# Features of keys and queries: one fp32 row-tile product of unsplit numbers in place of three terms of rounded parts

## What is computed

```python
q = einsum('bsd,dhk->bhsk', x, wq)      # 16 heads of 32; k and v alike
def _phi(u, omega):                     # omega: 128 x 32
    proj = einsum('bhsk,mk->bhsm', u, omega)
    sq = 0.5 * sum(u * u, axis=-1, keepdims=True)
    stab = max(proj, axis=-1, keepdims=True)
    return exp(proj - sq - stab) / sqrt(m) + 1e-06
pq, pk = _phi(q * scale, omega), _phi(k * scale, omega)
kv = einsum('bhsm,bhsk->bhmk', pk, v);  z = sum(pk, axis=2)
out = einsum('bhsm,bhmk->bhsk', pq, kv) / einsum('bhsm,bhm->bhs', pq, z)
```

## Time and profile before

| what | value |
|---|---|
| median of 3 runs | 3481.13 us (3478.57 to 3484.28) |
| the profiled execution, its span | 3482.2 us (1.1 us above the median, inside the three) |
| PE busy | 3422.0 us, 98% |
| weight loads (PEld) busy | 3151.9 us, 91% |
| DVE / ACT / POOL busy | 71% / 57% / 32% |
| mean granted TensorE clock | 0.993 of full speed |
| DMA queue's packets | 34.6% of 16 engines' span |

### The profile page before, as it was taken

One profiled execution on the slowest core, in us unless ns is written; L12 is line 12 of the kernel. 1 busy time (PEld: TensorE's weight loads), 2 busy tenths in 40 slices (PEclk: granted clock), 3 DMA queues, 4 the chain that ended last, 5 costly groups with the idle time before them and its releaser, 6 DMA issues.

```text
span 3482.2 us, 77456 instructions
## 1 busy us (share of the span) xinstructions
PE 3422.0 (98%) x29993; PEld 3151.9 (91%) x29993; DVE 2468.2 (71%) x4839; ACT 1969.8 (57%) x4240; POOL 1105.2 (32%) x861
## 2 busy tenths in 40 slices
PE   8999999999899999999999999999999999999998
PEld 6888888888788888888888889999999999999998
DVE  6767777677667777677777766666666666666666
ACT  6777777777556666666656654444444444444443
POOL 3554554545345454555555532000000000000000
PEclk9999999999899999999999999999999999999999
DMA  3222222222323333232332346444444444444443
GB/s 128 80 77 74 95 77 83 77 74 77 107 79 114 106 102 115 82 126 94 102 109 93 111 144 206 147 148 148 147 146 146 146 146 146 146 146 146 146 147 126
DMA packets 195355, 409.83 MB, mean 118 GB/s; under 512 B 27440, under 2 KB 52528, under 8 KB 194992
## 3 DMA queue, kind: packets, MB, share of 16 engines
q1 hardware_dynamic: 194992, 404.89, 34.6%
HBM read 292.50 MB, written 112.33 MB: 116 GB/s over the span
## 4 chain that ended last, share of the span: by engine, by line
PE 70%; DVE 2%; ACT 1%; issue 0%; POOL 0%; DMA 0%; ACTq 0%; POOLq 0%; DVEq 0%
PE ffn_hidden L175 30%; PE attend_gated L175 20%; PE ffn_result L175 8%; PE attend_num L175 6%; PE attend_feat L1425 3%; PE attend_feat L1445 1%; PE ffn_turn L1910 1%; PE attend_turn L1415 1%; DVE attend_kvz_lo L1393 1%; DVE attend_pT_lo L1354 1%; PE attend_feat L1452 1%; PE attend_turn L1434 0%; ACT attend_kvz_hi L1300 0%; DVE attend_kvz_lo L1396 0%; DMA ffn_r_in<-in_L_attn_w_dram 0%
## 5 line engine op out<-in xcount | busy, mean ns | idle before, releaser
L175 PE MATMUL ffn_hidden<-ffn_yT_hi,ffn_wa_hi 128*128 128x256 f32 x2048 | 574.1, 280 | 3.5 <-DVE ffn_wa_lo L1798 1.8
L175 PE MATMUL ffn_hidden<-ffn_yT_lo,ffn_wa_hi 128*128 128x256 f32 x2048 | 573.3, 280 | 0.0
L175 PE MATMUL ffn_hidden<-ffn_yT_hi,ffn_wa_lo 128*128 128x256 f32 x2048 | 572.0, 279 | 0.0
L316 POOL TENSOR_TENSOR ffn_n_rstd<-ffn_n_base,ffn_n_power 128x2 f32<-128x2 f32 x32 | 27.5, 860 | 1300.1 <-DVE ffn_n_negmean L311 1300.1
L1780 ACT ACTIVATE ffn_ht_hi<-ffn_hs 128x512 fp32r<-128x512 f32 x248 | 156.4, 631 | 420.6 <-DVE ffn_hs L1827 420.6
L175 PEld LDWEIGHTS ffn_hidden<-ffn_yT_hi,ffn_wa_hi 128*128 128x128 f32 x2048 | 385.0, 188 | 4.4 <-DVE ffn_wa_lo L1798 2.3
L175 PEld LDWEIGHTS ffn_hidden<-ffn_yT_hi,ffn_wa_lo 128*128 128x128 f32 x2048 | 385.2, 188 | 0.0
L175 PEld LDWEIGHTS ffn_hidden<-ffn_yT_lo,ffn_wa_hi 128*128 128x128 f32 x2048 | 384.9, 188 | 0.2
L635 POOL TENSOR_TENSOR keys_z_sum<-keys_z_sum,keys_e 128x512 f32<-128x512 f32 x192 | 259.6, 1369 | 232.9 <-ACT keys_e L703 232.9
L1831 DVE TENSOR_TENSOR ffn_ht_lo<-ffn_hs,ffn_ht_hi 128x512 fp32r<-128x512 f32 x248 | 173.6, 700 | 218.9 <-ACT ffn_ht_hi L1780 218.9
L1765 ACT ACTIVATE ffn_hid<-ffn_hidden,ffn_bias 128x256 f32<-128x256 f32 x496 | 206.1, 467 | 180.5 <-PE ffn_hidden L175 180.5
(11 more groups left out here) (305 smaller groups left out, 11669.3 us busy)
## 6 DMA issues: line engine op xcount, KB each, us to landing
ffn_tq<-part_d SPq DMA_DIRECT2D x248, 512.0 KB, 3.9
keys_xin<-in_L_attn_x_dram SPq DMA_DIRECT2D x32, 512.0 KB, 4.5
xn_d<-keys_xn SPq DMA_DIRECT2D x32, 512.0 KB, 3.0
xT_d<-keys_xT_whole SPq DMA_DIRECT2D x32, 512.0 KB, 2.6
u_d<-keys_uq SPq DMA_DIRECT2D x32, 512.0 KB, 3.1
shared_xTf<-xT_d SPq DMA_DIRECT2D x32, 512.0 KB, 6.0
shared_uq<-u_d SPq DMA_DIRECT2D x32, 512.0 KB, 4.9
r_d<-shared_gate SPq DMA_DIRECT2D x32, 512.0 KB, 3.1
```

What stands on the lines that cost most here:

```text
L175: last = pe.matmul(out, stationary[a], moving[b], start=start and n == 0, stop=stop and n == len(TERMS) - 1)
```

## The change

`kT`, `qT` and `omT` become single fp32 tensors. Each three-term product of features becomes one product of fp32 operands, with the same stationary and moving shapes and the same order over c and j. The turned keys are copied once, by DVE (a copy in the place of the subtraction, which now itself waits for the turn on PE and for the `proj` that read `kT` last); ACT's copy is gone. The turned queries are copied once, by ACT in its old place; DVE's subtraction is gone. `omT` is copied once. All other products stay as they are, L1452 (`pick`) too.

```diff
@@ ACT, keys pass
-            act.activation(omT.hi[:, :], turn[:, 0:M], ACT.Copy).then_inc(omega_rounded, 1)
+            act.activation(omT[:, :], turn[:, 0:M], ACT.Copy).then_inc(omega_ready, 1)
...
-                if job == "turn_k":
-                    for j in range(HC):
-                        wait(act, feat[j].full, TG * g)
-                    act.wait_ge(k_turned, 2 * g + n + 1)
-                    act.activation(kT.hi[:, 2 * n:2 * n + 2, :], turn_halves, ACT.Copy).then_inc(kT_hi, 1)
@@ DVE, keys pass
-            dve.wait_ge(omega_rounded, 1)
-            dve.tensor_tensor(omT.lo[:, :], turn[:, 0:M], f32(omT.hi[:, :]), ALU.subtract).then_inc(omega_ready, 1)
...
                 if job == "turn_k":
-                    dve.wait_ge(kT_hi, 2 * g + n + 1)
-                    dve.tensor_tensor(kT.lo[:, 2 * n:2 * n + 2, :], turn_halves,
-                                      f32(kT.hi[:, 2 * n:2 * n + 2, :]), ALU.subtract).then_inc(k_split, 1)
+                    for j in range(HC):
+                        wait(dve, feat[j].full, TG * g)
+                    dve.wait_ge(k_turned, 2 * g + n + 1)
+                    dve.tensor_copy(kT[:, 2 * n:2 * n + 2, :], turn_halves).then_inc(k_split, 1)
@@ PE, keys pass, job proj
-                        for k, (x_, y_) in enumerate(TERMS):
-                            for j in range(HC):
-                                last = pe.matmul(feat[j].t[:, c * M:(c + 1) * M],
-                                                 kT[rows(j), c, n * P:(n + 1) * P][x_], omT[rows(j), :][y_],
-                                                 start=k == 0, stop=k == 2)
+                        for j in range(HC):
+                            last = pe.matmul(feat[j].t[:, c * M:(c + 1) * M], kT[rows(j), c, n * P:(n + 1) * P],
+                                             omT[rows(j), :], start=True, stop=True)
@@ ACT, attend pass
-                    act.activation(qT.hi[:, 2 * n:2 * n + 2, :], turn_halves, ACT.Copy).then_inc(qT_hi, 1)
+                    act.activation(qT[:, 2 * n:2 * n + 2, :], turn_halves, ACT.Copy).then_inc(q_split, 1)
@@ DVE, attend pass
-                if job == "turn_q":
-                    dve.wait_ge(qT_hi, 2 * g + n + 1)
-                    dve.tensor_tensor(qT.lo[:, 2 * n:2 * n + 2, :], turn_halves, f32(qT.hi[:, 2 * n:2 * n + 2, :]),
-                                      ALU.subtract).then_inc(q_split, 1)
@@ PE, attend pass, job max: as proj, with qT; job feat:
-                        for k, (x, y_) in enumerate(TERMS):
-                            for j in range(HC):
-                                if c == 0 and k == 0:
-                                    pe.wait_ge(feat[j].free, 4 * g + 2 + n)
-                                pe.matmul(feat[j].t[:, cols], omT[rows(j), :][y_], qT[rows(j), 2 * n + c, :][x],
-                                          start=k == 0, stop=False)
+                        for j in range(HC):
+                            if c == 0:
+                                pe.wait_ge(feat[j].free, 4 * g + 2 + n)
+                            pe.matmul(feat[j].t[:, cols], omT[rows(j), :], qT[rows(j), 2 * n + c, :], start=True, stop=False)
```

More of the change, by code:

```diff
@@ L878, in do @@
                     for c in range(NC):
[L879 to L885 removed]
+                        for j in range(HC):
+                            last = pe.matmul(feat[j].t[:, c * M:(c + 1) * M], kT[rows(j), c, n * P:(n + 1) * P],
+                                             omT[rows(j), :], start=True, stop=True)
+                            if c == NC - 1:
+                                last.then_inc(feat[j].full, 1)
                 if job == "kv":
@@ L1420, in do @@
                     for c in range(NC):
[L1421 to L1429 removed]
+                        for j in range(HC):
+                            if c == 0:
+                                wait(pe, feat[j].free, 4 * g + n)
+                            last = pe.matmul(feat[j].t[:, c * M:(c + 1) * M], qT[rows(j), c, n * P:(n + 1) * P],
+                                             omT[rows(j), :], start=True, stop=True)
+                            if c == NC - 1:
+                                last.then_inc(feat[j].full, 1)
                 if job == "below":
```

70 lines of the change are left out of this document (28 added, 42 removed), and 6 rows, old and new, of tables (FFN_OVER, KEYS_OVER).

## The result

The changed kernel takes 3435.27 us (median of 4 runs, 3434.16 to 3437.23); the kernel before, on the same chip, 3482.7 us (4 runs, 3478.57 to 3487.75). The ratio is 0.9868, with a 95% interval of 0.9854 to 0.9882: 47.4 us less of the medians, 41 to 51 by the interval. Two later executions, both of the kernel with two copies (experiment 5), ran at a mean granted clock of 0.85 and 0.56 and took 3680 and 5528 us; they are left out of its median and ratio.

What follows compares the result with a forecast made beforehand. The prediction took PE's own instructions to bound the keys and attend passes. Its terms, -57.3 + 12.8 - 2.0 - 0.3 = -46.8 us from the profiled 3482.2 us, gave 3435.4, written as 3435 us, range 3402 to 3474.

Steps and rivals of the forecast that it cites:

- PE bounds both passes: In the keys and attend passes PE's own instructions set the time: busy 808 of 810 and 1084 of 1090 us.
- 128 columns, -57.3 us: `proj` and `max` (L881, L1425): a chunk costs 0.224 us in place of 0.336, over 512 chunks, -57.3 us.
- 256 columns, +12.8 us: `feat` (L1445): two fp32 records of 0.23 us make a chunk 0.46 in place of 0.36, over 128 chunks, +12.8 us.
- Copies and waits, -2.0 us: Keys pass: without ACT's copy the chain PE waits for shortens; of PE's 3.3 us of waits, 2 are given back.
- the start, -0.3: Start of the kernel: one small subtraction fewer, -0.3 us.
- Rival 1, pairs in single file: Row-tile products: strict program order makes a product's second record hold up the next head; +129 us, 3609 us, chance 0.13.
- Rival 2, the gain of `max` is not kept: Attend pass: waits for feature banks lose L1425's half of the 57.3 us; 3464 us, chance 0.10.
- Rival 3, 256 columns at 0.12 a record: `feat` (L1445): an fp32 record costs 0.12 us, not 0.23; 3407 us, chance 0.09.
- Rival 4, a chunk at 0.315 us: 128-column products: partly held up pairs at about 0.315 us a chunk leave no gain; 3482 us, chance 0.04.

Runs made afterwards that it cites:

- experiment 5: The changed kernel with ACT's copy of the turned keys back, into a buffer nothing reads, and DVE's copy waiting for it: 3439.38 us, ratio 0.9876.
- Experiments 1 and 2: 1: kernel before with only keys (`proj`) fp32, 3456.54 us. 2: changed kernel with keys pass as before, only queries (`max`, `feat`) fp32, 3458.11 us.
- experiment 3: The changed kernel with loops of `proj` and `max` exchanged, heads outside and chunks inside, eight records of a head in a row: 3648.8 us, ratio 1.0471.
- experiments 6 to 8: 6: kernel before, fp32 keys, `max` only hi by hi, 3420.92 us. On it, 7: second `r` before the turn, 3482.16; 8: second `max` before first `k`, 3474.61.
- experiment 4: The changed kernel with `proj` and `max` ordered as two chunks (four records) of each head in a row, then the other two: 3454.81 us, ratio 0.9918.

## Why the prediction was right, point by point

**The total** was right, 3435 against 3435.27, and the chance went where it belonged. That it came out to 0.3 us is luck. The two large terms were each too large: together they gave -44.5 us and measured -42.0. The copies and the start, for which 2.3 us were given, show no net gain. What closed the gap is 6.8 us that the sum did not have, more than half of it from the clock, which the sum took as unchanged. Also, 3435.4 was the sum for the profiled execution, which took 3433.4; less the 1.1 us that were named, it would have been 3434 for the median.

- *PE bounds both passes*. Right. PE's busy time and the span fell by the same 49 us.
- *128 columns, -57.3 us.* The mechanism is right, the size is 0.85 of it: 48.8. The step of 0.112 us is exact, eight in place of twelve. The term mis-sized is the entry: the pass was to be 8 x 0.112 + 0.24 = 1.14 us and is 1.19, since the first step of fp32 takes 0.214 us (491.616 to 491.830) where the first step of three terms took 0.16 (504.59 to 504.75). 0.052 us x 128 = 6.7 us, and the heads' 7 ns stagger makes 1 more. Experiments 1 and 2 show the term in its halves.
- *256 columns, +12.8 us.* 6.8 were measured. The record takes 0.217 to 0.224 us (1226.105 to 1226.329), so my 0.23 was 0.01 high, and a chunk costs 0.08 more, not 0.10: the second `feat` of a group is 2 x 0.08 longer (1.249 to 1.409). The first is only 0.08 longer (1.426 to 1.506); why it gives half of it back was not tried. The Trainium skill (FP8 and Floating Point Precision, Matmul Precision, TensorE Precision Notes) counts four passes for fp32; at 256 columns these records agree, two of 0.22 us to a product where an fp32r one takes 0.12. At 128 columns a product costs only twice an fp32r one, 0.224 against 0.112.
- *Copies and waits, -2.0 us, and the start, -0.3.* The term was mis-sized; as a net gain it does not show. By the list of waits 3.3 became 2.4 us for the keys, but the waits for `xT_lo` rose from 3.2 to 4.6. From the start to the 5th `proj` the change gains 0.4 us, where its passes alone are 1.2 shorter. Experiment 5 shows the price of a second copy in the changed kernel, 0.9 us in the trace and 3 to 4 in the medians, all that the trace shows at the start of the keys pass. That ACT's and DVE's shorter lists are worth nothing elsewhere is right.
- *Rival 1, pairs in single file.* It did not come, and experiment 3 shows how near it was: with eight records of one head in a row the same pass takes 2.83 us, worse than three terms. The change escapes since its order has only two. The Trainium skill (TensorE: Matmul & The Clock Gate, Part 3, The mechanism) has matmuls start strictly in program order; here the ninth record starts 0.33 us ahead of the eighth, so for products of different rows the measurement decides against it.
- *Rival 2, the gain of `max` is not kept.* It is kept in the change (24.7 us). It is what happens one step further, in experiments 6 to 8.
- *Rival 3, 256 columns at 0.12 a record.* No: 0.217 at the least. *Rival 4, a chunk at 0.315 us*, falls with the step of 0.112: a chunk is 0.224.
- *What the sum did not have.* 6.8 us of the 48.8. The largest piece, 3.7 us, is between the first and the 5th `max`, and it is the clock's. Busy time and mean granted clock over 120 us that begin 11 us before the last `proj` pass, of before (first fence) and of the change (second; columns as in the earlier trace rows):

```profile
870.00:990.00 120.00, 103.11 (x926) 92.95 (x923) 78.07 (x129) 63.12 (x138) 48.86 (x38) 0.86 0.31 96
```

```profile
846.00:966.00 120.00, 101.09 (x825) 88.42 (x826) 81.14 (x135) 67.73 (x147) 49.26 (x39) 0.93 0.34 109
```

The clock has two levels here, 1.2 and 2.4 GHz. With 0.86 the kernel before spent 34 us of this stretch at the lower one, with 0.93 the change 17 us. PE was busy for 86% and 84% of it, less than in any stretch of the earlier trace rows, for in it one pass drains and the next fills. The traces show where that counts. Of the stretches at the lower level that before has here, the last, 955.0 to 965.3 us, has none beside it in the change. The same window, counted from the first `max`, and neighbouring records of the same twelve `num` products, of before and of the change:

```profile
955.00:965.30 10.30, 8.91 (x75) 8.60 (x76) 4.33 (x8) 2.58 (x5) 7.15 (x6) 0.50 0.48 167
956.96 0.41 PE L175 MATMUL attend_num<-attend_pT_hi,attend_kvz_lo 128*128 128x256 f32 x1
957.17 0.41 PE L175 MATMUL attend_num<-attend_pT_hi,attend_kvz_hi 128*128 128x256 f32 x1
```

```profile
930.20:940.50 10.30, 9.43 (x121) 8.96 (x122) 4.25 (x8) 4.16 (x7) 7.24 (x7) 1.00 0.45 158
931.38 0.28 PE L175 MATMUL attend_num<-attend_pT_hi,attend_kvz_lo 128*128 128x256 f32 x1
931.50 0.28 PE L175 MATMUL attend_num<-attend_pT_hi,attend_kvz_hi 128*128 128x256 f32 x1
```

These products start every 0.21 us before and every 0.12 us in the change. The twelve take 2.83 us (change: 1.60), the `max` pass behind them 2.76 (1.10, of which the change itself makes 0.39), and the twelve `num` products after that 2.72 (1.53). That is 1.2 + 1.3 + 1.2 = 3.7 us. The other traces go with it: the changed kernel, its repeat, the two with two copies and the queries' half have no lower stretch there and take 75.3 to 75.6 us from the first to the 5th `max`. The keys' half (78.8 us) and the order with two chunks in a row (78.7) have one of 7 us, the order with the heads outside (81.5) one of 14. So this part of the gain is the clock's, shown by the same records at both levels. That it comes with fp32 queries is not shown: two other orders of the same fp32 records have a lower stretch there too. Why the chip grants the full clock there in one kernel and half of it in another is open.

The remaining 3 us are pieces of about 1 us, two of them in the products between the passes (L175: 438.8 to 437.7 us in 56 `proj` passes, 775.6 to 774.6 in 56 `max` passes). The first comes with either half of the change alone (437.4 with the queries' half, whose keys pass is that of before) and stays with two copies in turn, so it is neither `proj`'s products nor ACT's copy; its cause is open.

## What to carry to other kernels

Cost a small matmul by the distance between starts, not by its recorded duration, and count records: here a step of four 32-row records of 128 columns costs 0.112 us, whatever the number type, so fp32 with two records beats three fp32r terms at 128 columns, and at 256 columns, where the fp32 record costs 0.22 against 0.12, it loses. When row tiles share the array, keep the products of one row tile apart in program order: the same 32 records took 1.19, 1.31 or 2.83 us. And when a pass bound by one engine is made shorter, look at the engine that reads its output: 57 us taken from `max` were worth 36, and two moves meant to fill one wait cost 54 and 61 us, a part of it by a lower clock. Look at the granted clock of each stretch before a difference is put down to products or waits.

## What the hardware showed that I had not expected

- A record on other rows can start ahead of waiting ones, but in the order with eight of a head in a row never more than three were passed: the ninth started with the fifth, the seventeenth with the thirteenth (experiment 3).
- With four of a head in a row a step of 0.11 us is lost in the second half of each pass (experiment 4), unexplained.
- Entering fp32 row tiles costs more than entering fp32r ones: 0.214 us to the second record of 128 columns against 0.16, and 0.32 to the second of 256 columns (1225.785 to 1226.105), where later ones come after 0.22.
- Between the keys pass and the attend pass the clock is at its lower level for 17 to 34 us in twelve traces, and the two traces of the unedited change differ by 3 us (17.1 and 20.5). In the kernel before PE was busy for all of 840 to 860 us and for 16.1 of the 20 us from 870 to 890, at a granted clock of 1.00; from 890 to 910 it was 0.74. In the 120 us of this stretch PE was busy for 84 to 88% of the time.
- At the lower level the same records start about twice as far apart: 0.21 us against 0.12 for 256 columns of fp32r.
